# An online-softmax accumulator kept in 32x32-block-transposed layout on one Trainium2 core

## The reference, cut to what matters

```python
q = (M @ Wq.T).reshape(512, 8, 64).transpose(1, 0, 2)          # 512 queries, 8 heads of 64
k, v = jnp.split(x @ Wkv.T + bkv, 2, axis=-1)                  # 6250 keys, same heads
sim = jnp.einsum('hid,hjd->hij', q, k) * 64 ** -0.5
sim = jnp.where(mask, sim, -1e9)
attn = jax.nn.softmax(sim, axis=-1)
out = jnp.einsum('hij,hjd->hid', attn, v)                      # -> (512, 512)
m = layer_norm(out @ Wo.T + bo + M)
ffn = jax.nn.relu(m @ W1.T + b1) @ W2.T + b2                   # 512 -> 2048 -> 512
z = layer_norm(ffn + m)
```

## Time and profile before

| | us |
|---|---|
| median of 3 runs | 691.82 |
| lowest and highest | 691.11, 695.0 |
| the profiled execution | 695.23 |
| its span, first to last instruction | 693.1 |
| share of the span in which VectorE, ScalarE, GpSimd are busy | 79%, 52%, 37% |
| mean granted TensorE clock | 0.975 of full |

### The profile page before, as it was taken

The page is one execution under the profiler, slowest core; times in us unless marked ns, Lnnn a source line. Parts: engine busy times, 40 slices in busy tenths (PEclk is TensorE's granted clock), DMA queues, the critical chain, the costliest instruction groups (busy, mean ns, idle before and its releaser), DMA issues.

```text
span 693.1 us, 11140 instructions
## 1 busy us (share of the span) xinstructions
PE 635.1 (92%) x3382; PEld 398.1 (57%) x3382; DVE 549.6 (79%) x685; ACT 363.5 (52%) x659; POOL 254.5 (37%) x312
## 2 busy tenths in 40 slices
PE   4899999899999999998999999999998796999994
PEld 3666455555665555655555565545653344788883
DVE  3779999989998999898998999899998726333334
ACT  4566555655655665554665555656564313333322
POOL 3541642265224532263225522363212405422223
PEclk9899999999999999999999999999999799799998
DMA  8058888979898888887887989889786981032221
GB/s 286 3 150 216 226 219 219 238 177 221 220 238 200 221 211 236 211 205 193 210 232 192 216 209 248 210 200 219 189 203 177 256 238 65 30 110 101 91 61 61
DMA packets 56105, 128.36 MB, mean 185 GB/s; under 512 B 15856, under 2 KB 20976, under 8 KB 55792
## 3 DMA queue, kind: packets, MB, share of 16 engines
q1 hardware_dynamic: 45296, 101.97, 57.4%
q10 hardware_dynamic: 10752, 25.70, 14.3%
HBM read 23.80 MB, written 1.05 MB: 36 GB/s over the span
## 4 chain that ended last, share of the span: by engine, by line
PE 48%; DVE 17%; SPq 12%; issue 8%; DMA 5%; ACT 4%; POOL 2%; ACTq 2%; DVEq 1%; POOLq 0%
PE tail L920 12%; SPq L376 11%; PE slot L876 10%; DVE st L731 9%; PE slot L973 6%; PE slot L981 6%; PE tail L802 5%; PE slot L802 5%; DVE prob L721 5%; DMA pt<-st 3%; ACT prob L567 2%; ACTq L618 2%; PE tail L929 2%; DMA wq_raw<-in_wq 1%; PE slot L834 1%
## 5 line engine op out<-in xcount | busy, mean ns | idle before, releaser
L567 ACT ACTIVATE prob<-prob,negmax 128x896 f32<-128x896 f32 x224 | 233.5, 1043 | 206.8 <-DVE negmax L721 191.7
L721 DVE CUSTOM_DVE_ANT_0 prob<-slot,lower,negmax_old 128x896 f32<-128x896 f32 x224 | 249.0, 1149 | 41.9 <-PE slot L876 29.7
L731 DVE STREAM_TRANSPOSE st<-prob 128x1792 f32<-128x1792 f32 x112 | 228.6, 2041 | 6.2 <-DMA pt<-st 5.9
L920 PE MATMUL tail<-pt,val 128*64 128x512 f32 x784 | 186.9, 613 | 7.8 <-ACT outT_sb L597 5.4
L920 PEld LDWEIGHTS tail<-pt,val 128*64 128x64 f32 x784 | 52.8, 139 | 103.8 <-issue 94.8
L876 PE MATMUL slot<-k_hi,q_hi 64*128 64x448 f32 x448 | 95.8, 418 | 13.0 <-DVE negmax L721 6.8
L876 PEld LDWEIGHTS slot<-k_hi,q_hi 64*128 64x128 f32 x448 | 43.8, 185 | 80.8 <-issue 68.9
L876 PE MATMUL slot<-k_hi,q_lo 64*128 64x448 f32 x448 | 84.8, 366 | 0.0
L876 PE MATMUL slot<-k_lo,q_hi 64*128 64x448 f32 x448 | 84.4, 365 | 0.0
L456 POOL TENSOR_TENSOR total<-total,alpha 128x8 f32<-128x8 f32 x28 | 5.8, 206 | 195.4 <-ACT alpha L622 195.3
L477 POOL TENSOR_TENSOR k_lo<-k_raw,k_hi 128x896 fp32r<-128x896 f32 x27 | 57.1, 2114 | 3.9
(11 more groups left out here) (117 smaller groups left out, 836.6 us busy)
## 6 DMA issues: line engine op xcount, KB each, us to landing
pt<-st SPq DMA_DIRECT2D x672, 112.0 KB, 3.1
pt<-st ACTq DMA_DIRECT2D x224, 112.0 KB, 3.4
w_raw<-in_w SPq DMA_DIRECT2D x32, 256.0 KB, 2.8
x_raw<-in_x SPq DMA_DIRECT2D x13, 448.0 KB, 4.1
mask_raw<-in_mask SPq DMA_DIRECT2D x7, 448.0 KB, 4.3
mt_raw<-in_mt SPq DMA_DIRECT2D x2, 512.0 KB, 8.2
wo_raw<-in_wo SPq DMA_DIRECT2D x1, 1024.0 KB, 7.4
m_res<-in_mn SPq DMA_DIRECT2D x1, 1024.0 KB, 5.1
```

What stands on the lines that cost most here:

```text
L567: nc.scalar.activation(unit, unit, ACT.Exp, bias=negmax[:, p, u:u + 1], scale=-1.0, accum_out=psumrow[:, p, u:u + 1]).then_inc(exp_done, 1)
L721: nc.vector.tensor_tensor_reduce(out=prob[:, i % 2, h].rearrange("p (b n) -> p b n", b=2), in0=slot[:, j, :, :HALF], in1=lower[:, i].rearr ...
L731: nc.vector.transpose(st[:, g].rearrange("p b k (t i) -> p k b t i", t=2)[:, :, :, t2], prob[:, i % 2].rearrange("p h (k b i) -> p (h k) b ...
L920: last = nc.tensor.matmul(outT[DH * h:DH * h + DH], val[:, val_at(i, parity ^ (p < 0)), head(p, h)], moving, start=(i == 0), stop=(i == KT ...
```

## The change

The accumulator keeps the layout in which a 32x32-block transpose of `outT` arrives: dimensions and queries are exchanged within blocks of 32 only. In a block, a partition is a query and the 32 neighbouring elements of a row are dimensions of one head, so that a factor is needed for each partition and block, `[128, 16]` for a pair.

- `C` becomes one VectorE transpose of `outT` (PSUM) into `outT_sb`, 128x512. `F` is gone from TensorE. `A` is an addition of `outT_sb` to `acc` on GpSimd, and directly behind `C`; for the last two pairs it stays on VectorE.
- Both stand in the fourth round now. `A` takes the same pair as `C`, one pair-visit sooner than before.
- `Z` on ScalarE: behind `alpha` come 16 exponentials of 32 partitions by 4 elements each, which read a quadrant (32 partitions) of `drop` and write a quadrant of `alpha_blk`. GpSimd's scaling of `acc` waits for all 16.
- At the end `i` makes the reciprocal and spreads it with 16 VectorE copies of the same shape, `N` multiplies by it, and `G` is one VectorE transpose that also puts the blocks in order. The steps stand in another order: `Y` of the first two pairs follows the `W` of the third pair as a whole.

```diff
-     'S E0 E1 F W4 W5 W6 C A X M0 Q',
-     'S E0 E1 V2 X B0'),
+     'S E0 E1 W4 W5 W6 X M0 Q',
+     'S E0 E1 V2 C A X B0'),
...
-    acc = sb("acc", [P, PAIRS, QT, P], F32)
+    acc = sb("acc", [P, PAIRS, BLOCKS, LANES], F32)
+    alpha_blk = sb("alpha_blk", [P, PAIRS, BLOCKS], F32)
...
+        def quadrants():
+            for dims in range(QUAD):
+                for queries in range(QUAD):
+                    yield dims, queries, dims // 2
+        def block_stat(stat, p, dims, queries):
+            own = stat[LANES * dims:LANES * dims + LANES, p]
+            return own.rearrange("p (g q t) -> p q g t", g=2, q=QUAD)[:, queries]
+        def tile_stat(stat, p, queries, h):
+            own = stat[LANES * queries:LANES * queries + LANES, p, QT * h:QT * h + QT]
+            return own.rearrange("p (g t) -> p g t", g=2)
...
 # GpSimd, Z
-  nc.gpsimd.tensor_tensor(by_head(acc[:, own]), by_head(acc[:, own]), per_head(alpha, own), ALU.mult).then_inc(acc_scaled, 1)
+  pool.wait_ge(alpha_blk_ready, blocks)
+  nc.gpsimd.tensor_tensor(acc[:, own], acc[:, own], per_block(alpha_blk, own), ALU.mult).then_inc(acc_scaled, 1)
+ # GpSimd, A
+  pool.wait_ge(acc_scaled, posed)
+  pool.wait_ge(outT_copied, posed)
+  nc.gpsimd.tensor_tensor(own, own, by_block(outT_sb[:]), ALU.add).then_inc(acc_added, 1)
...
 # ScalarE: C is removed; Z
   nc.scalar.activation(alpha[:, p % PAIRS], drop[:, p % PAIRS], ACT.Exp).then_inc(alpha_ready, 1)
+  for dims, queries, h in quadrants():
+      nc.scalar.activation(block_stat(alpha_blk, p % PAIRS, dims, queries), tile_stat(drop, p % PAIRS, queries, h),
+                           ACT.Exp).then_inc(alpha_blk_ready, 1)
...
 # VectorE: A is removed for all but the last two pairs
+  if kind == "C":
+      dve.wait_ge(acc_added, read)
+      dve.wait_ge(pv_done, done)
+      nc.vector.transpose(by_block(outT_sb[:]), by_block(outT)).then_inc(outT_copied, 1)
+  if kind == "i":
+      nc.vector.reciprocal(inv[:, p], total[:, p]).then_inc(inv_ready, 1)
+      for dims, queries, h in quadrants():
+          nc.vector.tensor_copy(block_stat(alpha_blk, p, dims, queries), tile_stat(inv, p, queries, h)).then_inc(inv_blk_ready, 1)
+  if kind == "G":
+      nc.vector.transpose(ao_raw(p).rearrange(...), acc[:, p].rearrange(...)).then_inc(ao_ready, 1)
...
 # TensorE: F and G are removed
-  for t in range(QT):
-      last = nc.tensor.transpose(tp[:, P * t:P * t + P], outT_sb[:, P * t:P * t + P], ident[:])
-  last.then_inc(f_filled, 1)
```

More of the change, by code:

```diff
@@ L42 @@
 LANES = P // QUAD
+BLOCKS = E // LANES
 PAIR_LANDED = 16 * QUAD * QUAD
@@ L119, in chunk_schedule @@
                 out.append(step)
-                if kind == "A" and last and step[1] >= 0:
-                    out.append(("N", step[1], 0))
     if last:
         a, b = PAIRS - 2, PAIRS - 1
-        out.extend([("F", 1, 0), ("A", 1, 0), ("N", 1, 0)])
         out.extend([("X", b, 3), ("M", b, 1), ("B", b, 1), ("Z", b, 0), ("I", b, 1), ("O", b, 1)])
[L126 to L132, removed]
+        out.extend([("i", 0, 0), ("N", 0, 0), ("G", 0, 0), ("i", 1, 0), ("N", 1, 0), ("G", 1, 0)])
+        out.extend([("T", 0, 0), ("D", 0, 0), ("T", 1, 0), ("D", 1, 0), ("i", a, 0)])
+        out.extend([*(("W", a, kt) for kt in range(KT)), ("C", a, 0), ("A", a, 0), ("N", a, 0), ("G", a, 0), ("T", a, 0), ("D", a, 0)])
+        out.extend([*(("Y", 0, t) for t in range(QT)), ("i", b, 0)])
+        out.extend([*(("W", b, kt) for kt in range(KT)), ("C", b, 0), ("A", b, 0), ("N", b, 0), ("G", b, 0), ("T", b, 0), ("D", b, 0)])
+        out.extend([*(("Y", 1, t) for t in range(QT)), *(("Y", 2, t) for t in range(QT))])
     return out
@@ L469, in body @@
                             nc.gpsimd.tensor_tensor(wv2[1][:], wv_raw[:], wv2[0][:], ALU.subtract).then_inc(wv_lo, 1)
+                    if kind == "A" and not (final and p >= PAIRS - 2):
+                        posed, own = in_register(pool, pair_no(c, p) + 1), acc[:, p % PAIRS]
+                        pool.wait_ge(zeroed, 2)
+                        pool.wait_ge(acc_scaled, posed)
+                        pool.wait_ge(outT_copied, posed)
+                        nc.gpsimd.tensor_tensor(own, own, by_block(outT_sb[:]), ALU.add).then_inc(acc_added, 1)
                     if kind == "L":
@@ L590, in body @@
                                              ACT.Identity, bias=bk_sb[:, p % PAIRS:p % PAIRS + 1]).then_inc(drained[KEYS_RING], 1)
[L591 to L598, removed]
                     if kind == "T":
-                        act.wait_ge(aoT_filled, p + 1)
-                        nc.scalar.activation(ao2[0][:, p], gather_bank(p), ACT.Identity, bias=bv_sb[:, p:p + 1]).then_inc(aohi, 1)
+                        act.wait_ge(ao_ready, p + 1)
+                        nc.scalar.activation(ao2[0][:, p], ao_raw(p), ACT.Identity, bias=bv_sb[:, p:p + 1]).then_inc(aohi, 1)
                     if kind == "B":
@@ L733, in body @@
                             prob[:, i % 2].rearrange("p h (k b i) -> p (h k) b i", b=QUAD, i=LANES)).then_inc(xposed, 1)
-                    if kind == "A":
+                    if kind == "C":
+                        read, done = in_register(dve, n) if is_past(n, 1) else None, in_register(dve, KT * (n + 1))
+                        dve.wait_ge(zeroed, 2)
+                        if read is not None:
+                            dve.wait_ge(acc_added, read)
+                        if isinstance(n, int) and n == 0:
+                            dve.wait_ge(qlo_done, PAIRS)
+                        dve.wait_ge(pv_done, done)
+                        nc.vector.transpose(by_block(outT_sb[:]), by_block(outT)).then_inc(outT_copied, 1)
@@ L735, in body @@
+                    if kind == "A" and final and p >= PAIRS - 2:
                         dve.wait_ge(acc_scaled, n + 1)
[L736 to L739, removed]
+                        dve.wait_ge(outT_copied, n + 1)
+                        nc.vector.tensor_tensor(acc[:, p], acc[:, p], by_block(outT_sb[:]), ALU.add).then_inc(acc_added, 1)
@@ L936, in body @@
                                 pe.wait_ge(drained[j], emptied[j] + 1)
-                        if p >= 2:
-                            pe.wait_ge(aolo, p - 1)
-                        for t in range(QT):
-                            last = nc.tensor.transpose(gather_bank(p)[:, P * t:P * t + P], acc[:, p, t], ident[:])
-                        last.then_inc(aoT_filled, 1)
-                    if kind == "Y":
-                        if p == 0 and i == 0:
                             pe.wait_ge(wohi, 1)
```

58 lines of the change are left out of this document (30 added, 28 removed), and 14 rows, old and new, of the table ROUNDS.

## The result

The changed kernel takes 755.04 us (median of 4 runs, 751.97 to 758.53), the kernel before 692.97 in the same comparison: a ratio of 1.089, with an interval of 1.085 to 1.094. Forecast were 687.5 us and a range of 679 to 704. Even the rival that named the right mechanism, "ScalarE's block is held" with 702.9, is 52 us short.

A forecast was written before the change was run, and what follows sets the result against it. VectorE and TensorE, whichever is late at each hand-over, were taken to bound the loop. 695.23 - 6.4 (loop) + 2.1 (end) = 690.9 us profiled, 3.4 above the median: 687.5 us, 80% range 679 to 704.

The forecast's parts named there:

- ScalarE's block is held: Rival, 28%: at a pitch of 0.20 the 16 exponentials delay keys' bias and split; chunk 75.8, in all 702.9 us.
- the cost of the block in the loop: ScalarE's 16 exponentials between `alpha` and the keys' bias: 1.6 us a block at pitch 0.10, costing nothing.
- Which engines are close, and what the order gives: Attention loop: VectorE 72.2 us a chunk, TensorE 68.5; with 1.2 us of waits 73.4, 1.0 less, 6.4 us gained.
- I take 0.10, the row that shows two neighbours: Start-to-start pitch of ScalarE's small exponentials, taken from `alpha` and the next instruction; 1.6 us in a block.
- the turning point: Loop: the pitch of about 0.15 at which the slack of the keys' split is gone and the block starts to cost.
- Each pair keeps some 0.4 us: Held-block rival, loop: delay left in each pair, about 1.5 in the third; 2.3 to 2.7 a chunk above the forecast.
- the split's 0.8 us of slack: Loop, GpSimd: the split of the keys ends at 261.7, the next pair's scores needing it start at 262.54.
- The queue behind the block: Behind the block wait keys' bias, four DMA issues and next exponentials on ScalarE, scaling of `acc` and keys' split on GpSimd.
- The end: After the loop: VectorE's copies start the last value steps 3.0 us later, 0.9 regained after them; costs 2.1 us.
- 0.19 a copy: End, VectorE: each of 16 small copies costs a small reciprocal's duration; 3.0 us a group, low bound 0.10 a copy.
- Nothing in the loop: Rival, 20%: removed transposes were covered by VectorE, or block landing holds the period; chunk stays 74.4, 693.9 us.
- VectorE bound, fully: Rival, 16%: the whole rest above VectorE's own sum goes; chunk 72.2, in all 679.8 us.

The follow-up runs named there:

- with one exponential: The changed kernel with one ScalarE exponential of 128x16 in place of the 16 small ones, output not the reference's: 693.13 us, 1.000 of the kernel before.

## Why the prediction was wrong

The step that failed is the cost of the block in the loop, which was put at nothing. By the last score's start it costs 62.3 us (596.79 in the changed kernel, 534.54 with one exponential). For the profiled execution the forecast was 690.9 and 751.97 was measured, 61.1 more: 62.3 for the block and 5.7 at the end, less 5.2 that the loop gained beyond the forecast and 1.4 behind the end, within 0.3.

- **Which engines are close, and what the order gives: right.** Without the block the chunk is 72.8 us (forecast 73.4), with VectorE at 94.9% and TensorE at 94.9%. The loop's gain without it was 11.6 us, not 6.4. The new transpose takes 0.64 from start to start (0.77 taken), the GpSimd addition lasts 1.28, and with one exponential nothing is seen to wait for it.
- **"I take 0.10, the row that shows two neighbours": the term that was mis-sized.** Those neighbours had no change of quadrant, nor has the first of a block behind `alpha`; the other 15 have one. The pitch is 0.227, above even the bound of 0.20, which took the duration of an instruction for the cost of one that is held. That alone turns "a block costs nothing" into 3.6 us. The condition itself was not refuted: blocks of 1.5 and 1.9 us cost nothing, those of 3.6 us do, the turning point was put at 2.4.
- **The rival's price, 75.8 a chunk: right mechanism, under a quarter of the size.** Against the forecast's chunk it added 2.4 us; against the chunk with one exponential it is 83.6 - 72.8 = 10.8. "Each pair keeps some 0.4 us" was wrong: each keeps 1.5 to 1.9 (19.45 against 17.9 at the least). That VectorE, at 94.9%, has no room to catch up is my reading of it. And in the third pair the text named the value copy and the two value projections but not `J0`, which stands on GpSimd between the scaling and the split: there the split's 0.8 us of slack does not exist (even with one exponential TensorE waits for `k_lo` there once a chunk, up to 0.87 us), and the pair keeps 4.5 or more.
- **The queue behind the block.** The prediction listed the four DMA issues and then priced only the bias and the split. That they are a limit of their own showed once the other two were freed.
- **The end: +2.1 forecast, +7.8 measured.** 0.19 a copy holds only for a group without GpSimd beside it. The first two groups, priced at 3.0 us each, took 4.72 and 3.78 in the changed kernel, and the first projection began 21.1 us behind the last score instead of 18.9. It took 8.2 us up to the last value steps instead of 5.7: its first ten products followed a pause of 8.70 us at a granted clock of 0.50, 0.43 us apart instead of 0.23. Of these 8.2 us only 0.35 were a wait for the transpose behind the third group, though that group had stretched to 7.39. From there to the last projection it was 11.7 instead of 10.7, mostly because the fourth group, which had no term, was still running as the value steps ended. That is 2.2, 2.5 and 1.0 us more.
- **"Nothing in the loop" and "VectorE bound, fully"** are out for the kernel as it is. Without the block the chunk of 72.8 lies halfway between the second's 72.2 and the forecast.

How much of the loop's 50.7 us the lower clock makes was not isolated; the kernel before with the block loses 52.0 us there at a clock of 0.98 from 200 to 300 us.

## What to carry to other kernels

Price a run of small instructions by the start-to-start distance of a row with the same pattern of quadrants; where they alternate, take a little more than the full duration of each (here 0.227 for 0.20). Then ask what stands behind the run on its in-order engine, DMA issues included, and follow each item to its own limit: cut the run in pieces and put them where none of these items is queued, since an engine at 65% can hold up two at 95% by place alone. If both neighbours are nearly full, little of a delay is caught up: here 1.5 us or more of it stayed in every pair. At the end of a kernel, ask of each long instruction whether the engine behind it would have been free any sooner.

## What was not expected of the hardware

- ScalarE holds an instruction that begins in another quadrant, by source or by target: 0.227 us from start to start for 4 elements on 32 partitions, against 0.12 with three changes in 16 and 0.093 with none (128 partitions, 1 element).
- 16 small VectorE copies took 3.04 us alone and 7.1 to 7.4 beside a GpSimd instruction of 4.5 to 4.6 us, a single copy among them 4.4 to 4.5; an addition of 128x512 with both inputs in SBUF 4.42 instead of 0.69. Transposes and score products of VectorE kept their durations throughout (0.71, 2.00 to 2.05 and 1.15 us).
